# An attention and hash-routed expert kernel: the expert tiles that start early, in one stage of five or in two of four and three

## The reference, cut to what matters

```
x  = layernorm(x + attention(x))          # x: 4 x 512 tokens of 128
h  = mod(int(x[:, 0] + x[:, 1]), 8)        # the token's expert; its second one is h+1 mod 8
for e in range(8):                         # E = 8 experts, F = 512
    w = any([h, (h+1) % 8] == e) / 2
    acc += w * (relu(x @ W1[e] + b1[e]) @ W2[e] + b2[e])
out = layernorm(x + acc)
```

## Time and profile before

| | |
|---|---|
| runs | 242.27, 242.37, 243.25 us (median 242.37) |
| profiled execution, its time | 244.44 us |
| its span, first to last instruction | 242.4 us (2.0 us lie around it) |
| instructions | 9670 |
| busy: PE, DVE, ACT, POOL | 88%, 61%, 50%, 48% of the span |
| attention loop, passes 0 to 15 | to about 126.3 us |
| draining passes and first full tile's up products | 126.3 to 142.5 us |
| full tiles | to about 161.9 us |
| loop over the remaining 17 tiles, on PE | 161.9 to 232.3 us |
| last output transfer issued | 236.5 us |

### The profile page before, as it was taken

One profiled execution on the slowest core, in us unless ns is written; L12 is line 12 of the kernel. 1 busy time (PEld: TensorE's weight loads), 2 busy tenths in 40 slices (PEclk: granted clock), 3 DMA queues, 4 the chain that ended last, 5 costly groups with the idle time before them and its releaser, 6 DMA issues.

```text
span 242.4 us, 9670 instructions
## 1 busy us (share of the span) xinstructions
PE 213.6 (88%) x3473; PEld 180.2 (74%) x3473; DVE 149.1 (61%) x522; ACT 122.2 (50%) x364; POOL 117.0 (48%) x218
## 2 busy tenths in 40 slices
PE   7879999998999899999996689997999999899930
PEld 6536777865887678867775489896899999799920
DVE  7735467786577876887998325264655564555640
ACT  2625757765577755765663146642434445235410
POOL 6453034762544438663847311457556453545551
PEclk9988999999999999999999979999999999999985
DMA  3231120023222233300101535422121212112100
GB/s 98 56 91 46 47 91 3 6 86 89 89 54 73 59 100 99 101 14 7 35 14 48 129 107 170 130 54 57 34 65 44 54 40 58 27 36 46 34 22 7
DMA packets 18552, 14.67 MB, mean 61 GB/s; under 512 B 2646, under 2 KB 15546, under 8 KB 18512
## 3 DMA queue, kind: packets, MB, share of 16 engines
q1 hardware_dynamic: 17008, 11.83, 18.3%
q0 software_dynamic: 1216, 2.16, 2.8%
q10 hardware_dynamic: 288, 0.13, 0.2%
HBM read 11.43 MB, written 3.03 MB: 60 GB/s over the span
## 4 chain that ended last, share of the span: by engine, by line
PE 52%; DMA 13%; issue 12%; DVE 9%; ACT 3%; SPq 3%; POOL 3%; DVEq 2%; POOLq 1%; ACTq 0%
DMA out<-yo,idx 11%; PE bT L1249 7%; PE bS L1300 4%; PE bV L1264 4%; PE bS L1188 4%; PE bS L1217 3%; PE bJ L1164 3%; PE bV L1271 2%; PE bS L1231 2%; PE bL L1357 2%; PE bV L1444 2%; PE bV L1451 2%; PE bJ L1122 2%; DVEq L304 1%; PE bL L1375 1%
## 5 line engine op out<-in xcount | busy, mean ns | idle before, releaser
L680 ACT ACTIVATE ha<-bS,b1c 128x128 f32<-128x128 f32 x68 | 19.4, 368 | 41.5 <-PE bS L1300 41.5
L668 ACT COPY PTs<-bT 128x512 f32<-128x512 f32 (+3 forms) x48 | 25.9, 539 | 17.5 <-PE bT L1249 17.3
L566 POOL DMA_INDIRECT out<-yo,idx x18 | 19.1, 1061 | 17.3 <-POOL idx L562 11.5
L1300 PE MATMUL bS<-xsT,w_s 128*128 128x128 f32 x204 | 26.4, 279 | 1.1 <-issue 1.1
L1249 PE MATMUL bT<-ident,Pr 128*128 128x128 f32 x168 | 27.2, 279 | 0.1
L1300 PEld LDWEIGHTS bS<-xsT,w_s 128*128 128x128 f32 x204 | 24.1, 192 | 2.3 <-issue 2.2
L497 POOL TENSOR_SCALAR rstd<-mv 128x1 f32<-128x1 f32 x16 | 3.8, 234 | 43.8 <-DVE mv L859 43.8
L513 POOL DMA_INDIRECT groups<-x,pos x16 | 16.5, 1034 | 13.5 <-DVE pos L909 10.2
L1249 PEld LDWEIGHTS bT<-ident,Pr 128*128 128x128 f32 x168 | 19.9, 146 | 4.0 <-issue 3.6
L655 ACT ACTIVATE Pr<-bS 128x512 f32<-128x512 f32 x32 | 20.1, 627 | 2.8 <-PE bS L1231 2.8
L814 DVE TENSOR_REDUCE mx<-bS 128x8 bf16<-128x512 f32 x32 | 21.4, 677 | 0.0
(11 more groups left out here) (237 smaller groups left out, 506.8 us busy)
## 6 DMA issues: line engine op xcount, KB each, us to landing
w_s<-in_L_ffn_W SPq DMA_DIRECT2D x16, 256.0 KB
w1f<-in_L_ffn_W SPq DMA_DIRECT2D x10, 256.0 KB
xrow<-groups SPq DMA_DIRECT2D x22, 64.5 KB, 2.0
xs<-groups SPq DMA_DIRECT2D x18, 64.0 KB
x_tok<-in_L_attn_x SPq DMA_DIRECT2D x4, 256.0 KB, 3.2
groups<-padrows SPq DMA_DIRECT2D x1, 516.0 KB, 5.7
b2r<-in_L_ffn_b SPq DMA_DIRECT2D x1, 512.0 KB, 3.8
out<-yo,idx POOLq DMA_INDIRECT x18
```

What stands on the lines that cost most here:

```text
L566: nc.gpsimd.indirect_dma_start(rows_out, bass.IndirectOffsetOnAxis(ap=idx[:], axis=0), yo[:, FULL - 1, :], None, bounds_check=T * P - 1, o ...
L668: nc.scalar.copy(PTs[:, j, 0:m, :], bT[:, 0:m * P].rearrange("p (c q) -> p c q", c=m)).then_inc(turned_out, 1)
L680: nc.scalar.activation(dst[:, c, :], src[:, c * P:(c + 1) * P], ACT.Relu, bias=bias_of(c)).then_inc(relu, 1)
L1300: last = mm(bank_of(c)[:, c * P:(c + 1) * P], w[:, c * P:(c + 1) * P], xsT[:], start=True, stop=True)
```

## The change

There are now two stages of full tiles. The first is decided after 11 token tiles (4 tiles), the second after 14 (3 more): seven full tiles, 15 in the loops. The chunks are 4, 4, 3, 3 and 2 token tiles. `base` holds each expert's first row not yet taken.

- The marks and places of chunk 2 move from pass 15 to the end of pass 13 and to pass 14; chunk 1 is scattered in pass 13 as a whole, chunk 2 at the start of POOL's pass 15. `full_tiles` of stage 1 comes into pass 15 of DVE, ahead of its row maxima.
- The draining passes are written out by hand and interleaved with the first full tiles, without idle transposes; the last tile's projections use bank bT. The marks of chunk 3 are split in three around `normalise(15)` and `residual(14)`, ahead of the last tile's work. The down products have a bank of their own, bF.
- Experts (`full_ok`) and rows (`full_row_ok`) are published apart. Each half of W1 has a buffer and a semaphore of its own; no load waits for another.
- b2 is halved once (`b2h`), and POOL adds it to the rows of x ahead (`xb`), so DVE needs one instruction fewer for each tile and no expert number; in the loops DVE adds it before the down product ends. ACT now copies out all seven sums.
- The last tile's layernorm is done by POOL as a whole again.

```diff
-    EARLY = T - KT_
-    FULL = (EARLY * P - E * (P - 1) + P - 1) // P
+    STAGES = [T - KT_ - 1, T - 2]
+    FIRST, FULL = (sure(n) for n in STAGES)
...
+            def load_full_weights(j, s):
+                sp.dma_start(w1f[:, j, s, :].unsqueeze(1),
+                             W1[bass.ds((experts[j] + s) % E, 1)].rearrange("e p f -> p e f")).then_inc(w1f_in[j][s], 16)
+
+            experts = []
+            for stage, js in enumerate(members):
+                for j in js:
+                    experts += load_table(sp, full_table[:, 0, :], [j], full_ok, E - 1, count=stage + 1)
+                    load_full_weights(j, 0)
+                    row, = load_table(sp, full_table[:, 1, :], [j], full_row_ok, E * SEG - P, count=stage + 1)
+                    sp.wait_ge(scattered, 16 * STAGES[stage])
+                    sp.dma_start(xrow[:, j * XW:(j + 1) * XW], seg[bass.ds(row, P), :]).then_inc(full_in[j], 16)
+                    load_full_weights(j, 1)
...
+            def biased_rows(js):
+                for j in js:
+                    expert, = load_table(pool, full_table[:, 0, :], [j], full_ok, E - 1, count=1 if j < FIRST else 2)
+                    pool.wait_ge(full_in[j], 16)
+                    nc.gpsimd.tensor_tensor(xb[:, j, :], xrow[:, j * XW:j * XW + D], b2f[:, bass.ds(expert * D, D)],
+                                            ALU.add).then_inc(xb_ok, 1)
+            layernorm(T - 3)
+            biased_rows([0, 1])
+            layernorm(T - 2)
+            biased_rows([2, 3])
+            scatter(3, chunks[3], scattered)
+            layernorm(T - 1)
+            scatter(LAST, chunks[LAST], scattered_late)
+            biased_rows(members[1])
...
+            turned_attention(T - 2)
+            up_full(0, 1)
+            turned_remote(T - 1)
+            project(T - 2)
+            columns(1)
+            down_full(0, 0)
+            remote(T - 1)
+            up_full(1, 0)
+            rank_late(3)
...
-                nc.vector.scalar_tensor_tensor(y2[:, s, :], ysum[:], 0.5, xk, ALU.mult, ALU.add).then_inc(y_ok, 1)
+                nc.vector.scalar_tensor_tensor(y2[:, s, :], f, 0.5, xk, ALU.mult, ALU.add).then_inc(y_ok, 1)
...
-                    pe.wait_ge(biased, k)
+                    pe.wait_ge(y_ok, k)
```

More of the change, by code:

```diff
@@ L1078, in _ @@
                     dve.wait_ge(kept, k * 16 + 16)
+                    nc.vector.tensor_tensor(ysum[:], xrow[:, bass.ds(k * XW, D)], b2h[:, e, :], ALU.add).then_inc(biased, 1)
                     dve.wait_ge(down, k + 1)
[L1080 to L1081 removed]
+                    dve.wait_ge(biased, k + 1)
+                    moments(k, FULL - 1, bY[:, 0:D], ysum[:])
             dve.wait_ge(table_ok, 1)
```

497 lines of the change are left out of this document (253 added, 244 removed).

## The result

The changed kernel took 240.75 us (median of 6 runs, 239.1 to 242.31); the kernel before beside it 243.03 us (6 runs). The ratio is 0.9897, 95% interval 0.9857 to 0.9938: 2.3 us or 1.0% faster, where 5.0 us were forecast. The direction held, and the time lies inside the range given, but above the range of the case I held likeliest (235.5 to 239.3). Of the 3.4 us between forecast (237.4) and result, 0.7 lies in the starting point: the forecast was counted from a median of three runs, 242.37, and that of six is 243.03. Ratios here are taken over the executions that lie within about 1.5% of the fastest of their kernel.

A forecast was written before the change was run, and what follows sets the result against it. The prediction took a chain of waits ending in serial output stores as the bound, PE close beside. First store 160.1 + 13.5 + 57.9 put the last at 231.5, 5.0 us earlier; 242.37 less 5.0 gave 237.4 us, range 234.6 to 241.2.

The forecast's parts named there:

- the case I held likeliest: Whole kernel: the time comes as forecast, 235.5 to 239.3 us; chance 0.52.
- the step from the row numbers to tile 3's rows on POOL: SP's queue before POOL's scatter of chunk 3: 11.3 us, from 130.1 to 141.4.
- The mark, 2.1 us on PE: Attention loop: DVE's mark at the end of pass 13 costs 2.25 us, uncovered, adding 2.1 us on PE.
- Rival 1: PE's clock falls in the draining passes; end moves by 1.3 to 2.6, to 238.7 to 240.0; chance, with some lateness, 0.18.
- The clock after 135: Sign of being wrong: PE's clock at half its level after 135 us.
- SP issues the first row load at 131.1: SP's queue: experts read and half the weights issued before, so tile 0's row load goes at 131.1.
- Period and landing of the rows: SP's row loads: 2.8 us from one to the next, each landing 2.0 us after issue.
- Rival 2: SP floods its queue: rows at 151, end 9.6 later, 247; slower than before from 6.2 us of lateness; chance 0.07.
- Three biased rows at 1.1 each: POOL before the first store: adding three biased rows ends at 157.6 and costs 3.3 us in full.
- `columns(0)`, the table, the stores: PE's `columns(0)` at 134.9, DVE's table at 154.1, first store 160.1, serial store 173.6, then 15 steps of 3.86.
- Rival 4: More gain: the 4.21 us store transfer doesn't recur (-1.9), the mark partly hidden (-1); 234.5 to 235.5; chance 0.14.
- The sum: End of the store row: last store at 231.5 where it was 236.5, 5.0 us less.

The follow-up runs named there:

- quick chips: The chips of jobs 1 and 3, where the kernel before has a mean of 243.0 and 243.3 us; the first measurement's before, 243.1, is like them.
- warm: Changed kernel with 16 idle transposes on PE while it stands for the mark in pass 14: 239.3 us, 0.9836 of the kernel before.
- scatter first: Changed kernel with POOL's scatter of chunk 3 ahead of the biased rows of tiles 2 and 3: 238.53 us, 0.978 of before by means.
- rows first: Changed kernel with SP loading a stage's rows behind the first tile's weights, ahead of other tiles' weights: 235.84 us (0.9637 of before), again 238.48 us (0.9761).
- job 3: Runs on a third chip, a quick one; changed kernel there 242.02 us, 0.9812 of the kernel before, 0.993 by means.
- first measurement: The changed kernel's first six runs and first profile, beside the kernel before: 240.75 us, ratio 0.9897.
- job 1: Follow-up runs on one quick chip; changed kernel there 240.11 us, 0.9802 of the kernel before, 0.991 by means.
- SP free: Changed kernel without SP's waits for the probabilities of passes 12 to 15: 247.57 us, 0.9983 of the kernel before.
- before again: The kernel before, unchanged, run again for another profile: 243.26 us (0.9997) in job 1, 247.71 us (0.9991) in job 4.
- the changed one again: The changed kernel, unaltered, run again for a second profile: 240.11 us in job 1, 0.9802 of the kernel before.
- mending the orders: Changed kernel with SP's row loads and POOL's scatter and last layernorm moved ahead: 245.17 us (0.9911 of before, SP's waits also removed), 247.48 us (1.0009, waits kept).
- job 2: Runs on a slow chip, where the kernel before has a mean of 248.2 us; the unaltered changed kernel was not among them.
- job 4: Runs on another slow chip, kernel before mean 247.5 us; changed kernel there 248.85 us, 1.0051 of before, 1.003 by means.
- half bias alone: The kernel before with only the change's bias part (b2 halved once, added by POOL; DVE reads no expert numbers): 246.5 us, 0.9954 of before.
- slow chip: A chip of job 2 or job 4, where the kernel before has a mean of 248.2 and 247.5 us.
- both orders: Changed kernel with rows first, and POOL's chunk 3 scatter and last layernorm ahead of two biased rows: 247.48 us (1.0009); with idle transposes 244.16 us (0.9892).

## Why the prediction was right in direction and wrong in size

The step that failed is the one from the row numbers to tile 3's rows on POOL, which the prediction called what gates POOL: it gave SP's queue 11.3 us for it, and the runs show 13.6 to 14.8. The 2.6 us or more that are missing there arrive almost whole at the last store, and moving the weights behind the rows brings them back on quick chips (by means 5.2 and 2.9 us). The paragraphs on the first row load and on the period and landing of the rows take this step apart; the clock, which the sum left out too, comes first.

**The mark, 2.1 us on PE: right as a stall, mis-sized as a term.** The stall is 2.25 to 2.27 in every quick-chip profile with the mark in pass 13 but warm, where transposes fill it. But I costed a standing PE at its standing time. The clock fell behind it in four of the six quick-chip profiles with that stall (the changed kernel twice, scatter first, rows first in job 3; not in the first measurement nor in rows first of job 1), and where it was measured that cost 1.2 to 1.7 us. Rival 1 had the mechanism and the price (1.3 to 2.6) and put them in the wrong place, the draining passes; against it I held that PE never rests over 1.0 us there, which was so. The 2.1 us rest that I had myself added two passes earlier I never held against it. This step failed too, but an error the other way hid it: without the fall the row numbers come at 128.96 in an execution that starts like the forecast's (rows first, job 1), 1.1 us before the 130.1 of the forecast, and with it at 130.17. That they agreed to 0.1 is luck.

**The clock after 135.** The last sentence of the prediction named "PE's clock is at half its level after 135" as a sign of being wrong, and it is there in all three quick-chip profiles of the changed kernel: 0.50 in 152 to 154 in the first, 0.65 and then 0.50 in 152 to 156 in job 1, and 0.77 and 0.50 in job 3, behind waits of 3.15, 2.17 and 2.44 us for the last mark. A group of eight matmuls takes up to 2.03 instead of 1.06 there. The first store waits for POOL at that time and not for PE, so what it costs at the end isn't shown.

**SP issues the first row load at 131.1: 1.1 us too early.** "SP has read the experts and issued half the weights before" failed: SP was still at its wait on pass 15's probabilities until 130.03, 1.8 us behind the table. Whom a queue waits for ahead of the new code, I hadn't followed. With that wait taken out (SP free) the first row load gained the 1.1 us back, but tile 3's rows did not.

**Period and landing of the rows: 0.5 and 1.0 us too short.** 2.8 us was 2.97 on average (3.28 in the first profile), and a landing of 2.0, a median over rows mostly without weights ahead of them, was 2.98 with 256 KB before and behind. This is Rival 2 in small: 2.6 us of lateness at tile 3's rows, where it would have been slower than before from 6.2. Scatter first and rows first show that this wait decided what follows: 3.9 and 5.1 us at the first store, of which some 1.2 to 1.5 in rows first are the clock's; with the fall on both sides (job 3) it is 3.0.

**Three biased rows at 1.1 each: one waited 2.06 us for its own rows.** They cost 3.3 us as forecast in sum (156.59 to 159.92), though by other terms: two sums in 0.86, then the wait.

**`columns(0)`, the table, the stores: right.** The row numbers at 130.17 (130.1). The table at 155.92 (154.1) and the first store at 162.08 (160.1) late by what the rows were late. From the first store to the serial one 13.7 (13.5). Fifteen serial steps 58.3 (57.9).

**The slow transfer.** One store of the row, for whose landing POOL waits 1.5 to 2.9 us where it waits 0.6 for its neighbours, is in all eighteen profiles, at 203 in before again (2.18), at 184 in the changed one again (2.63): taking it as an accident of one execution (Rival 4) was wrong, and it belongs to neither side of the sum.

**The sum.** Laid beside an execution that had the same early fall, the last store came at 234.03, forecast 231.5: 2.5 us of the 5.0 missing, and the medians say 2.7. The times of the first profile agreed with the forecast to 0.5 us only because that execution started 2.2 us ahead. Had I judged by it, I would have called every step right. The range was also put together wrongly: by the chances given, 0.16 and not 0.1 lies above its upper end of 241.2, and next to nothing below 234.6.

**What stays open.** Why ScalarE stands 2.3 us longer at one place on two of four chips: no releaser of this core is shown, and I ran nothing that moves its instructions there. On those chips mending the orders brought less, 0.8% in job 2 (against SP free) and nothing that can be told in job 4 (0.997 [0.993, 1.002]), so the account of the missing 2.7 us is shown for the quick ones. Whether DVE's register reads had been on the path at all is open too: half bias alone, on a slow chip, brought a third of what was expected. Whether the first measurement's chip was a quick one is only inferred from its before.

A version ahead of both on quick chips is the changed kernel with the rows first (0.964 and 0.976, by means 0.970 and 0.981 of before). With both orders and the idle transposes it is 0.989 (0.986) on a slow chip, where the change itself gains nothing; that version wasn't run on a quick one.

## What to carry to other kernels

When a change makes TensorE stand in one piece, as for 2.3 us here, cost the clock behind the stand as well as the stand, and try a stretch of idle matmuls in it; splitting the wait kept the clock up here, but brought no time. When a new step stands in a DMA queue, follow the queue's older waits up to it, and put the small transfers that others wait for ahead of the large ones that nobody needs yet; it was worth 1.2 to 2.2% here on quick chips. And before a sum is made against one profiled execution, compare its early part, which the change doesn't touch, with another.

## What the runs showed of the hardware

- The granted clock falls in the first 20 us in 12 of 18 profiled executions, at one of two pairs of matmuls (6.43 or 16.05 us; up to 2.08 instead of 1.13), and what follows is some 2 us later (POOL's last copy of Kx at 104.3 to 105.6 instead of 102.7 to 103.0 on quick chips). It is a part of the spread between executions of one kernel, and lies in no code that was changed.
- One kernel's mean differs by 5 us between chips (243.0 and 243.3 against 247.5 and 248.2), and the ratio of two kernels differs as well: 0.991 and 0.993 against 1.003 for the same pair.
- A row load of 64.5 KB, 2.0 us to landing in the median of the kernel before, took 2.5 to 3.5 us with 256 KB loads on either side of it in the queue, and up to 4.13 with three other row loads close behind.
- ScalarE stood 4.57 to 4.82 us ahead of one copy in all six profiles with the mark in pass 13 on two chips, and 2.30 to 2.32 in those on the other two with the same code; no instruction of the core is shown as the releaser.
